# Opening of a convolution and FFN kernel: new order of ScalarE's and VectorE's steps, first input pair in two loads

## What is computed

```python
# x (32, 64, 1024)
out = lax.conv_general_dilated(x, weight, window_strides=(1,), padding=[(4, 4)], feature_group_count=4, ...)
x1 = out + einsum('nd,od->no', c, c_weight)[:, :, None] + bias[None, :, None]
...
w_up = (NF4[w_up_codes] * repeat(w_up_absmax, 64)).reshape(2752, 1024).T
y1 = x1 @ w_up + b_up + x1 @ w_up_lora_a @ w_up_lora_b
x2 = relu(y1)
w_down = (NF4[w_down_codes] * repeat(w_down_absmax, 64)).reshape(1024, 2752).T
x = x + x2 @ w_down + b_down + x2 @ w_down_lora_a @ w_down_lora_b
...
# second layer: softmax-weighted kernels per batch entry, then one of 8 experts per row
x = x + experts(conv1x1(x))
```

## Time and profile before

| what | value |
|---|---|
| median of the runs (lowest, highest) | 1441.71 us (1440.62, 1446.35) |
| span of the profiled execution | 1438.6 us |
| TensorE busy (matmul) | 1398.8 us, 97% |
| VectorE busy | 1137.8 us, 79% |
| ScalarE busy | 755.7 us, 53% |
| mean granted TensorE clock | 0.994 |
| TensorE on the chain that ended last | 85% of the span |

### The profile page before, as it was taken

One profiled execution on the slowest core, in us unless ns is written; L12 is line 12 of the kernel. 1 busy time (PEld: TensorE's weight loads), 2 busy tenths in 40 slices (PEclk: granted clock), 3 DMA queues, 4 the chain that ended last, 5 costly groups with the idle time before them and its releaser, 6 DMA issues.

```text
span 1438.6 us, 20752 instructions
## 1 busy us (share of the span) xinstructions
PE 1398.8 (97%) x6817; PEld 1146.1 (80%) x6817; DVE 1137.8 (79%) x1101; ACT 755.7 (53%) x839; POOL 211.0 (15%) x218
## 2 busy tenths in 40 slices
PE   7899999999999999999999999999999899999996
PEld 7888888888888888888888888887755688888785
DVE  6869887878877787887878878787644699999895
ACT  5655554545546455464554644643123277777672
POOL 0111000000000000000000000000011266665443
PEclk9999999999999999999999999999999999999998
DMA  6864656568665686656865667756668547969951
GB/s 221 315 223 165 236 209 254 196 250 273 237 246 203 234 292 229 227 218 227 294 240 206 240 220 281 256 191 240 238 231 287 160 121 194 354 190 303 332 146 35
DMA packets 102680, 331.48 MB, mean 230 GB/s; under 512 B 15220, under 2 KB 22908, under 8 KB 102620
## 3 DMA queue, kind: packets, MB, share of 16 engines
q1 hardware_dynamic: 79556, 258.56, 48.4%
q0 software_dynamic: 22816, 71.85, 17.9%
q10 hardware_dynamic: 256, 0.40, 0.1%
HBM read 295.63 MB, written 46.14 MB: 238 GB/s over the span
## 4 chain that ended last, share of the span: by engine, by line
PE 85%; DMA 6%; DVE 3%; issue 2%; ACT 2%; SPq 0%; ACTq 0%; POOL 0%; DVEq 0%; POOLq 0%
PE pair L1133 26%; PE pair L1135 26%; PE pair L1134 25%; PE pair L1187 4%; DMA z_rows<-z 3%; DMA wraw<-exp_w 3%; PE pair L1402 1%; DVE wf L808 1%; PE pair L1214 1%; PE pair L1271 1%; PE pair L1197 1%; ACT z L718 1%; DVE wlr L1108 1%; PE pair L1369 1%; PE pair L1183 1%
## 5 line engine op out<-in xcount | busy, mean ns | idle before, releaser
L808 DVE TENSOR_TENSOR wf<-wf,term 128x1024 f32<-128x1024 f32 x308 | 376.7, 1223 | 65.7 <-ACT term L593 50.5
L593 ACT ACTIVATE term<-codes 128x1024 f32<-128x1024 int32 x308 | 320.6, 1054 | 139.4 <-DVE wf L808 139.4
L1133 PE MATMUL pair<-wh,hh 128*128 128x512 f32 x672 | 263.4, 392 | 3.2 <-DVE ring L871 1.4
L1134 PE MATMUL pair<-wl,hh 128*128 128x512 f32 x672 | 262.0, 390 | 0.0
L1135 PE MATMUL pair<-wh,hl 128*128 128x512 f32 x672 | 262.0, 390 | 0.0
L1133 PE MATMUL pair<-ring,wh 128*128 128x512 f32 x656 | 255.5, 390 | 0.0
L1134 PE MATMUL pair<-ring,wh 128*128 128x512 f32 x656 | 255.3, 389 | 0.0
L1135 PE MATMUL pair<-ring,wl 128*128 128x512 f32 x656 | 255.2, 389 | 0.0
L741 ACT ACTIVATE whr<-wraw 128x1024 fp32r x184 | 187.9, 1055 | 85.3 <-PE pair L1135 50.8
L866 DVE TENSOR_TENSOR acc<-acc,pair 128x1024 f32<-128x1024 f32 x160 | 194.4, 1216 | 47.2 <-PE pair L1135 39.8
L1108 DVE TENSOR_TENSOR wlr<-wraw,whr 128x1024 fp32r<-128x1024 f32 x184 | 213.3, 1215 | 12.5 <-ACT whr L741 12.2
(11 more groups left out here) (178 smaller groups left out, 1527.6 us busy)
## 6 DMA issues: line engine op xcount, KB each, us to landing
ring<-x_parts SPq DMA_DIRECT2D x320, 512.0 KB, 6.4
wraw<-exp_w SPq DMA_DIRECT2D x64, 512.0 KB, 11.2
x_parts<-stage POOLq DMA_DIRECT2D x24, 512.0 KB, 6.0
xg<-exp_b POOLq DMA_DIRECT2D x23, 512.0 KB, 8.0
codes<-codes_up SPq DMA_DIRECT2D x22, 512.0 KB, 5.8
codes<-codes_dn SPq DMA_DIRECT2D x22, 512.0 KB, 5.6
am<-am_dn SPq DMA_DIRECT2D x22, 512.0 KB, 3.7
acc<-x_nat POOLq DMA_DIRECT2D x16, 512.0 KB, 5.5
```

The costliest lines, as they stand in the source:

```text
L593: return nc.scalar.activation(out, codes[:, n % 2], ACT.Relu, scale=scale, bias=-scale * bend)
L808: nc.vector.tensor_tensor(whole(n), whole(n), term[:, e % 2], op).then_inc(term_added, 1)
L1133: mm(ps, ah, bh, start=first, stop=False)
L1134: mm(ps, ah, bl, start=False, stop=False)
```

## The change

The order of ScalarE's and VectorE's steps on weight tiles 0, 1 and 2 among the 21 batches is another. ScalarE makes `head(0, 0)` and the first two ramps ahead of batch 0, VectorE the first add; from there on the steps stand one to three batches earlier than before, and VectorE's batches 3 and 9 and ScalarE's batch 8 hold one large step more than the others. VectorE's low part of tile 1 stands behind batch 18, and two more adds of tile 2 stand among the batches, with the ramps that they need. TensorE's two `lora_product` stand behind batches 5 and 13. SP loads the first input pair in two halves, the second behind the first codes; batch 0 waits for the first half on a new semaphore `first_in`, batch 1 for the second.

```diff
--- before.py
+++ after.py
@@ -254,6 +254,7 @@
         ctx_const, ctx_mm, ctx_split, mask_ready, ctxd_ready, tz_in = (sem(n) for n in (
             "ctx_const", "ctx_mm", "ctx_split", "mask_ready", "ctxd_ready", "tz_in"))
         xcv_in = [sem(f"xcv_in{i}") for i in range(4)]
+        first_in = sem("first_in")
         conv_mm, x1h_ready, x1l_ready = sem("conv_mm"), sem("x1h_ready"), sem("x1l_ready")
         x1_stored = [sem(f"x1_stored{i}") for i in range(NC)]
         acc_in = [sem(f"acc_in{i}") for i in range(NC)]
@@ -349,8 +350,9 @@
                     sp.dma_start(ring[:, kt].rearrange("p s t -> p (s t)").bitcast(F32),
                                  x1_dram[q % NC, kt]).then_inc(x1_in[kt], 16)
 
-            load_pair(0)
+            sp.dma_start(xcv0[:, 0], x_conv[:, 0]).then_inc(first_in, 16)
             load_codes(0, 0)
+            sp.dma_start(xcv0[:, 1], x_conv[:, 1]).then_inc(xcv_in[0], 16)
             load_pair(1)
             load_pair(2)
             load_lora(0, 0)
@@ -638,35 +640,38 @@
                 nc.scalar.activation(stages[c][:, :, 0, col:col + CH], bank[4 + k % 4].rearrange("p (j o) -> p j o", j=J),
                                      ACT.Copy).then_inc(x1h_ready, 1)
 
+            head(0, 0)
+            ramps(0, 0, (1, 2))
             for k in range(FIRST):
                 conv_high(k)
-                if k == 0:
-                    head(0, 0)
-                if k < 3:
-                    ramps(0, 0, (k + 1,))
-                elif k == 3:
+                if k < 2:
+                    ramps(0, 0, (k + 3,))
+                elif k == 2:
                     act.wait_ge(ffn_const, 32)
                     nc.scalar.activation(lora[:], lora_f[:], ACT.Copy).then_inc(lora_split, 1)
                     lora_high(0, 0)
-                elif k < 8:
-                    ramps(0, 0, (k,))
+                elif k < 6:
+                    ramps(0, 0, (k + 2,))
+                elif k == 6:
+                    head(0, 1)
+                elif k == 7:
+                    ramps(0, 1, (1,))
                 elif k == 8:
-                    head(0, 1)
-                elif k == 9:
-                    ramps(0, 1, (1,))
-                elif k == 10:
                     high(0, 0)
                     lora_high(0, 1)
-                elif k < 17:
-                    ramps(0, 1, (k - 9,))
+                    ramps(0, 1, (2,))
+                elif k < 14:
+                    ramps(0, 1, (k - 6,))
+                elif k == 14:
+                    head(0, 2)
+                elif k == 15:
+                    ramps(0, 2, (1,))
                 elif k == 17:
-                    head(0, 2)
-                elif k == 18:
-                    ramps(0, 2, (1,))
-                elif k == 20:
                     high(0, 1)
+                elif k in (18, 19):
+                    ramps(0, 2, (k - 16,))
             lora_high(0, 2)
-            ramps(0, 2, range(2, 8))
+            ramps(0, 2, range(4, 8))
             high(0, 2)
             relu(0, 0)
             for k in range(FIRST, LATE):
@@ -871,37 +876,43 @@
                 nc.vector.tensor_tensor(stages[c][:, :, 1, col:col + CH], bank[4 + k % 4].rearrange("p (j o) -> p j o", j=J),
                                         stages[c][:, :, 0, col:col + CH], ALU.subtract).then_inc(x1l_ready, 1)
 
+            add_ramps(0, 0, (1,))
             for k in range(FIRST):
                 conv_low(k)
                 if k < 3:
-                    add_ramps(0, 0, (k + 1,))
+                    add_ramps(0, 0, (k + 2,))
                 elif k == 3:
                     dve.wait_ge(lora_split, 1)
                     nc.vector.tensor_tensor(lora[RS:2 * RS], lora_f[RS:2 * RS], lora[RS:2 * RS],
                                             ALU.subtract).then_inc(lora_split, 1)
                     lora_low(0, 0)
-                elif k < 8:
-                    add_ramps(0, 0, (k,))
+                    add_ramps(0, 0, (5,))
+                elif k < 6:
+                    add_ramps(0, 0, (k + 2,))
+                elif k == 6:
+                    scale(0, 0)
+                elif k == 7:
+                    add_lora(0, 0)
                 elif k == 8:
-                    scale(0, 0)
+                    add_ramps(0, 1, (1,))
                 elif k == 9:
-                    add_lora(0, 0)
-                elif k == 10:
-                    add_ramps(0, 1, (1,))
-                elif k == 11:
                     low(0, 0)
                     lora_low(0, 1)
-                elif k < 18:
-                    add_ramps(0, 1, (k - 10,))
+                    add_ramps(0, 1, (2,))
+                elif k < 15:
+                    add_ramps(0, 1, (k - 7,))
+                elif k == 15:
+                    scale(0, 1)
+                elif k == 16:
+                    add_lora(0, 1)
+                elif k == 17:
+                    add_ramps(0, 2, (1,))
                 elif k == 18:
-                    scale(0, 1)
-                elif k == 19:
-                    add_lora(0, 1)
+                    low(0, 1)
                 else:
-                    add_ramps(0, 2, (1,))
-            low(0, 1)
+                    add_ramps(0, 2, (k - 17,))
             lora_low(0, 2)
-            add_ramps(0, 2, range(2, 8))
+            add_ramps(0, 2, range(4, 8))
             scale(0, 2)
             add_lora(0, 2)
             low(0, 2)
@@ -1172,7 +1183,9 @@
 
             def conv(k):
                 h, p = k // LATE, k // 2
-                if k % 2 == 0:
+                if k == 0:
+                    pe.wait_ge(first_in, 16)
+                elif k == 1 or k % 2 == 0:
                     pe.wait_ge(xcv_in[p % 4], 16 * (p // 4 + 1))
                 if k in (0, LATE):
                     pe.wait_ge(tz_in, 16 * (h + 1))
@@ -1289,10 +1302,10 @@
 
             for k in range(FIRST):
                 conv(k)
-                if k == 6:
+                if k == 5:
                     pe.wait_ge(lora_split, 2)
                     lora_product(0, 0)
-                elif k == 15:
+                elif k == 13:
                     lora_product(0, 1)
             up(0, 0, (0, 2)).then_inc(up_mm, 1)
             for k in range(FIRST, LATE):
```

## The result

The changed kernel takes 1435.53 us (median, 1432.88 to 1436.97), the kernel before beside it 1441.98 us. The ratio is 0.9945, with an interval of 0.9925 to 0.9965: 5 to 11 us less. A ratio here isn't the quotient of the medians shown beside it (0.9955 in the first comparison, 0.9944 in the second), but each interval holds both. The prediction was 1435.8 us, from a sum of 5.9 us.

The account below looks back on a forecast made before the run. TensorE's stand before up(0, 0), caused by VectorE's step order, and the half-rate clock behind it were taken as the loss to win. 3.93 + 1.63 + 0.3 = 5.9 us; 1438.6 - 5.9 + 3.1 = 1435.8 us, range 1433.9 to 1438.6.

Parts of the forecast that it names:

- The wait goes whole, 3.93 us: Before up(0, 0): the earlier low part of tile 1 ends TensorE's whole wait, 3.93 us, with 1.3 us margin.
- the lag of the crowded batches: VectorE's batches 3 and 9: lags of 1.3 and 1.2 us gone by batches 7 and 14; rival that they stay, 12%.
- The clock, 1.63 us: In up(0, 0): the half-rate stretch behind the stand goes, winning 1.63 us, or 0 if the clock falls for another reason.
- The opening, 0.3 us: At batch 0: with the first pair split, TensorE begins 0.64 us earlier, mostly at half rate, winning 0.3 us.
- The bounds of the term, -1.9 and +2.1: Opening: 2.1 us gained with batch 0 all at full rate; about 1.9 us lost if full rate comes one batch later.
- Half rate in batch 0: Batch 0 lost 1.42 us, meaning 2.84 us at half rate; full rate taken to come at about 11.45 regardless of start.
- The products moved up: TensorE's two lora products: the first, a batch earlier at 22.1, finds lora_low ready with 0.9 us cover; cost 0.
- No new wait in place of the old: Tile 2 behind batch 20: ends 4.9 us earlier, TensorE comes 5.9 earlier; rival that a new wait appears, 7%.
- one of the prediction's own signs of being wrong: At relu(0, 0): a relu that follows its high part without a pause would show the forecast wrong.
- the second reserve of that rival: Before conv_high(22): 1.16 us of waiting, used up after the 0.5 us before relu(0, 0) if tile 2 is late.
- Everything behind is tied to TensorE: Behind up(0, 0): everything hangs on TensorE, so the whole gain of 5 to 6 us should reach the end.
- its own rivals: Whole kernel: opening at full rate gives 1434.1 us (8%); the lag staying gives 1437.0 to 1438.7 us (12%).

Follow-up runs that it names:

- the two late low parts: The changed kernel with VectorE's low part of tile 1 one batch later, or two batches later; 1437.14 us (ratio 0.9968) and 1438.86 us (0.9982).
- before: The first profile of the kernel before, with nothing changed; profiled span 1438.6 us, median beside the changed kernel 1441.98 us.
- before_look: The kernel before, unchanged, profiled a second time for its clock and landings; no separate time given, up(0, 0) took 14.24 us.
- warm: The changed kernel with 8 matmuls of ones ahead of the context product and 4 behind it, during TensorE's wait for first loads; 1435.93 us, ratio 0.9964.
- table_later: The changed kernel with ScalarE's loads of the lora table and the biases issued behind its first step; 1434.15 us, ratio 0.9950.

## Why the prediction was right, step by step

- *The wait goes whole, 3.93 us.* Right. The stand is 3.92 us in all four profiles of the old order that leave it empty, and nought with the new. The margin came out as 1.30 us, the figure that was worked out, and the two late low parts stood for what that margin says. VectorE kept step, as reckoned: the lag of the crowded batches had gone before the low part, which started 0.61 us behind `conv_low(18)`.
- *The clock, 1.63 us.* The mechanism was right, and the size is right as a mean: 1.8 us over four profiles. As a constant it was wrong: the bounds 0 and 1.63 should have been 0 and 2.9, since one profile showed one draw. That this draw, 1.65, lay near the mean was luck. What the prediction cited from the Trainium skill for the opening ("TensorE: Matmul & The Clock Gate", Part 1, The HAM clock gate: the watched window runs freely) fits here as well: the same program with the same stand falls at another place, or not at all: in `before` half rate begins 1.3 us behind the start of `up(0, 0)`, in `before_look` with its first matmul. The window itself no run here shows.
- *The opening, 0.3 us.* This step failed: batch 2 began 0.42 us later in the profile after, not 0.3 earlier. Batch 0 began no earlier (0.09 us later), because `tz`, issued in front of the half pair, landed later. The DMA view (size, us from issue to landing) of the changed kernel:

```profile
tz<-toep SPq DMA_DIRECT2D x1, 512.0 KB, 5.5
...
xcv<-x_conv SPq DMA_DIRECT2D x1, 258.0 KB, 5.8
```

  `tz` landed 5.5 us after its issue, not 4.8, and the half pair 5.8 us after its own, as the whole pair had. The step took the landing of `tz` for fixed; over the profiles that load it in the old surroundings its wait is 4.7 to 5.8 us, with the pair whole as with the pair halved, and what half a pair saves (it lands 0.7 to 1.3 us behind `tz`, a whole pair 1.3 to 1.7) drowns in that. Over those profiles, `warm` left out, batch 2 begins at 14.07 to 16.06 with the pair whole (four, mean 14.99) and at 14.21 to 15.35 with it halved (six, mean 14.74): a gain of about the size that was reckoned is neither shown nor excluded. What held batch 0 was loads issued ahead of it, and `table_later` shows it: with ScalarE's two loads behind, 1.6 to 2.0 us. What of that is the table's 384 KB and what the small load of the biases wasn't separated, and it is more than the 0.7 to 1.0 us by which the landings were expected to move. The bounds of the term, -1.9 and +2.1, held.
- *Half rate in batch 0.* Right that it costs, and that its end isn't tied to batch 0's start; wrong in the release that the term took, a fixed moment (11.45 us). By the spacing of the matmuls full rate came at about 11.2 to 14.8 us, 3.0 to 6.0 us behind batch 0's start, in the twelve profiles without matmuls of ones there; in the profile after at about 12.4, and 0.33 of the 0.42 us come from that. Batches 0 and 1 lost between 1.42 and 2.86 us in those twelve. Of this the Trainium skill's rule, the same page and part, was the better guide, and the single row of before, 1.42, was the mildest of all draws.
- *The products moved up.* Right: `lora_low` ended at 21.68, TensorE used it at 22.55, 0.87 us of cover where 0.9 was reckoned.
- *No new wait in place of the old.* Right in the end, wrong on the way. A pause of 0.5 us before `relu(0, 0)` was left in the reckoning; in the profile the relu follows `high(0, 2)` with no pause (one of the prediction's own signs of being wrong), at 0.44 us behind the start of batch 21 where it was 0.28. One add was counted twice: behind `conv_low(20)` stand five adds in place of seven and no low part, three steps less and not four, so that `high(0, 2)` came 3.4 us earlier (65.59, 68.99 before) and not 4.9; the opening, 0.4 us later and not 0.3 earlier, took its part of that. The 0.16 us were taken up at `conv_high(22)`, whose pause went from 1.16 to 1.02, as the second reserve of that rival said.
- *Everything behind is tied to TensorE.* Right as far as the 1x1 convolution: from batch 21 to there 993.7 us before and 993.9 after. Behind it lies the spread of the routing and the experts, which the prediction didn't see and which a pair of single profiles can't see.

So 3.92 us and, on average, 1.8 make 5.7 of the 6.45 us between the medians; the rest lies well inside the interval. The sum came out at 5.9 with one term too many and one a little small; that the two nearly cancel is luck. The ends of the stated range, 1433.9 and 1438.6, lie 0.1 to 0.2 us beside the 1434.1 and 1438.7 that its own rivals give. The chances put 80% on a change within 0.5%: the first comparison gives 0.55%, the second 0.46%, each with an interval that holds both sides of the line.

## What to carry to other kernels

Where an in-order engine takes one step for each of another engine's batches, its spare time doesn't help a step with a deadline; the step's place in the order does, and each place is worth one batch of the other engine (2.02 us here), which can be checked by moving the step and reading the stand. A stand of TensorE can cost more than its length (up to 2.93 us more here), but the fall of the clock behind it is a draw, to be taken as a mean over several profiles. A stage far from the change can hide a gain in a pair of profiles (2.9 us here): compare mark by mark. Ahead of a halved first load, look first at what is issued before it: here that was worth 1.6 to 2.0 us, and the half's own gain was seen only with it out of the way (0.8 us, one profile of each).

## What the runs showed of the hardware

- The same stand of 3.92 us was followed by 0.03, 1.65, 2.73 and 2.93 us of loss at half rate; one of 2.79 by 1.6; those of 0.77 and of 1.41 by none.
- The granted clock of the opening reads 1.00 in the profile, while batch 0's matmuls begin 0.213 us apart and those of batch 2 0.112: the profile's share shows no fall before the first recorded one, and there the spacing must be read.
- Matmuls of ones from 1.95 us on didn't bring TensorE to full rate before batch 0: in `warm` the spacing changed at about 10.5 us, 1.9 us behind the start of batch 0. Why is open; no other data or kind of matmul was tried there.
